# Gates turned four units at a time on VectorE, b2's product over 128 zero-padded rows, TensorE's inserted transposes grouped

## The reference

```
HW   = layernorm(x) @ W                       # (8, 2048, 128)
A    = relu((adj + adj.T) / 2)                # (2048, 2048), symmetric
d    = A.sum(axis=1) ** -0.5
x1   = x + relu((I - d[:,None] * A * d[None,:]) @ HW)
z    = layernorm(x1)
p    = softmax(z @ router_w.T)                # 8 experts, the best 2 kept, made to sum to 1
out  = x1 + z + sum_e p_e * (gelu(z @ w1[e] + b1[e]) @ w2[e] + b2[e])
```

## Time and profile before

| | before |
|---|---|
| median of 3 | 950.52 us (948.55 to 951.11) |
| profiled execution | 949.63 us, span 947.9 us |
| mean granted TensorE clock | 0.986 of 2.4 GHz |
| TensorE products (PE) | 890.9 us busy, 94% |
| VectorE (DVE) | 645.9 us, 68% |
| ScalarE (ACT) | 516.9 us, 55% |
| GpSimd (POOL) | 311.3 us, 33% |
| stages | setup to about 87 us, graph to 542.7 us, experts to the end |

### The profile page before, as it was taken

One profiled execution on the slowest core, in us unless ns is written; L12 is line 12 of the kernel. 1 busy time (PEld: TensorE's weight loads), 2 busy tenths in 40 slices (PEclk: granted clock), 3 DMA queues, 4 the chain that ended last, 5 costly groups with the idle time before them and its releaser, 6 DMA issues.

```text
span 947.9 us, 15352 instructions
## 1 busy us (share of the span) xinstructions
PE 890.9 (94%) x4446; PEld 724.9 (76%) x4446; DVE 645.9 (68%) x1558; ACT 516.9 (55%) x899; POOL 311.3 (33%) x312
## 2 busy tenths in 40 slices
PE   4766799999999999999999989999999999999997
PEld 3765588888888788878888857777777777777775
DVE  3996634756867734152424288888888888888886
ACT  3665332344443321222122287888888888888885
POOL 0689335555574734474433430000000000000000
PEclk9997899999999999999999999999999999999999
DMA  9983255676485336867766774777777777777771
GB/s 286 327 253 125 98 202 212 255 270 215 166 290 175 102 139 251 281 245 262 267 246 239 286 253 163 263 265 266 267 269 270 270 270 270 270 270 270 270 269 45
DMA packets 93022, 222.98 MB, mean 235 GB/s; under 512 B 8856, under 2 KB 59568, under 8 KB 81072
## 3 DMA queue, kind: packets, MB, share of 16 engines
q1 hardware_dynamic: 86752, 211.59, 63.3%
q0 software_dynamic: 2560, 8.39, 2.3%
q10 hardware_dynamic: 3664, 2.43, 1.0%
HBM read 157.89 MB, written 64.49 MB: 235 GB/s over the span
## 4 chain that ended last, share of the span: by engine, by line
PE 81%; DVE 7%; POOL 4%; issue 4%; ACT 3%; DMA 1%; DVEq 0%; ACTq 0%; POOLq 0%
PE bank L913 11%; PE bank L915 11%; PE bank L914 11%; PE bank L1290 6%; PE bank L1293 6%; PE bank L1277 6%; PE bank L1279 6%; PE bank L1278 6%; PE bank L1291 6%; POOL col_sum L543 3%; PE bank L858 2%; PE bank L330 2%; DVE y_lo L699 2%; PE bank L1299 1%; PE bank L1287 1%
## 5 line engine op out<-in xcount | busy, mean ns | idle before, releaser
L1367 DVE TENSOR_TENSOR gated<-c_all,act_h 128x512 f32<-128x512 f32 x256 | 177.7, 694 | 46.2 <-ACT act_h L1329 41.6
L1329 ACT ACTIVATE act_h<-bank,b_sb 128x512 f32<-128x512 f32 x256 | 176.5, 690 | 58.5 <-PE bank L1279 54.0
L1372 DVE TENSOR_TENSOR g_lo<-gated,g_hi 128x512 fp32r<-128x512 f32 x256 | 175.7, 686 | 0.2
L1336 ACT ACTIVATE g_hi<-gated 128x512 fp32r<-128x512 f32 x256 | 159.1, 621 | 4.4 <-DVE gated L1367 4.4
L1262 POOL DMA_DIRECT2D out<-fin x32 | 24.3, 759 | 367.6 <-DVE fin L1380 362.9
L913 PE MATMUL bank<-y_hi,stage 128*128 128x512 f32 x256 | 111.3, 435 | 3.6 <-DVE y_lo L699 3.6
L1002 POOL TENSOR_TENSOR rstd<-var_eps,neg_half 128x4 f32<-128x4 f32 x32 | 48.8, 1525 | 179.5 <-DVE var_eps L1039 179.4
L1277 PE MATMUL bank<-z_e,w_hi 128*128 128x512 f32 x256 | 103.8, 406 | 1.7 <-ACT act_h L1329 1.5
L913 PE MATMUL bank<-y,stage 128*128 128x512 f32 x256 | 104.5, 408 | 0.0
L1293 PE MATMUL bank<-g_lo,w_hi 128*128 128x512 f32 x256 | 101.0, 395 | 2.9 <-DVE g_lo L1372 2.9
L1290 PE MATMUL bank<-g_hi,w_lo 128*128 128x512 f32 x256 | 103.7, 405 | 0.0
(11 more groups left out here) (118 smaller groups left out, 1582.1 us busy)
## 6 DMA issues: line engine op xcount, KB each, us to landing
c_all<-c_scratch SPq DMA_DIRECT2D x64, 1024.0 KB, 8.0
s_scratch<-stage SPq DMA_DIRECT2D x14, 2048.0 KB, 8.4
stage<-s_scratch SPq DMA_DIRECT2D x14, 2048.0 KB, 7.8
z_e<-z_scratch SPq DMA_DIRECT2D x32, 512.0 KB, 7.0
z_scratch<-z_hl SPq DMA_DIRECT2D x31, 512.0 KB, 2.7
x_raw<-in_x SPq DMA_DIRECT2D x32, 256.0 KB, 7.8
x_res<-in_x SPq DMA_DIRECT2D x32, 256.0 KB, 7.1
r_e<-res_scratch SPq DMA_DIRECT2D x32, 256.0 KB, 2.7
```

The source lines that it names most:

```text
L1329: act.activation(v.act_h[e % R][:, :], ps_h[e % 2][:, :], ACT.Gelu, bias=v.b1_sb[:, e:e + 1]).then_inc(gelu_done, 1)
L1336: act.activation(v.g_hi[e % R][:, :], v.gated[e % R][:, :], ACT.Copy).then_inc(hi_done, 1)
L1367: dve.tensor_tensor(out=v.gated[e % R][:, :], in0=v.c_all[s][:, e, :], in1=v.act_h[e % R][:, :], op=ALU.mult).then_inc(gated_done, 1)
L1372: dve.tensor_tensor(out=v.g_lo[e % R][:, :], in0=v.gated[e % R][:, :], in1=v.g_hi[e % R][:, :].bitcast(FP32), op=ALU.subtract).then_inc(lo ...
```

## The change

VectorE turns the gates itself. `gate_parts` is widened from 24 to 32 columns for each group, the last eight set to zero once by GpSimd. After `weigh` has made the gates of a batch, one `transpose` of VectorE turns the whole 128 x 512 tile in squares of 32 x 32 into `gate_x`. There the partitions 32g to 32g+23 hold the gates of the tokens 32g to 32g+31 of each group, so a run of tokens is only 32 long, 128 bytes. Sixteen stores for each batch (four units by four g, each of 24 x 4 runs) bring them to the same `c_dram`. SyncE issues them in unit 7, 11, ..., 31, ahead of `store_unit`, and GpSimd those of the last batch at the start of its expert stage. `turn_gate` and `copy_gate` and their entries in the tail lists are gone.

`b2_parts` and `c_parts` get 128 partitions; GpSimd sets all of them to zero once, in unit 20, and rows 0 to 23 are then filled as before. L1287 runs over 128 rows.

The inserts are moved: groups 0 and 1 from after steps 2 and 4 to after step 2, groups 2 and 3 from after steps 10 and 13 to after step 12, behind `turn_z`; `turn_x` from after steps 1 and 5 to after steps 2 and 6, the second one behind `project`.

```diff
-        v.gate_parts = sb("gate_parts", [P, T, 3 * E], FP32, at)
+        v.gate_parts = sb("gate_parts", [P, T, 32], FP32, at)
-        v.gate_t = [sb(f"gate_t{i}", [3 * E, CW], FP32, at) for i in range(2)]
+        v.gate_x = sb("gate_x", [P, T, 32], FP32, at)
-        v.b2_parts = sb("b2_parts", [3 * E, P], FP32R, at)
+        v.b2_parts = sb("b2_parts", [P, P], FP32R, at)
-        v.c_parts = [sb(f"c_parts{i}", [3 * E, CW], FP32R, at) for i in range(2)]
+        v.c_parts = [sb(f"c_parts{i}", [P, CW], FP32R, at) for i in range(2)]
...
+    def store_gates(eng, batch):
+        eng.wait_ge(gate_turned, batch + 1)
+        for u in range(4 * batch, 4 * batch + 4):
+            rows = v.c_dram[unit(u)].rearrange("e (q g t) -> g e q t", q=Q, g=4)
+            for g in range(4):
+                eng.dma_start(rows[g], v.gate_x[32 * g:32 * g + 3 * E, Q * (u % 4):Q * (u % 4) + Q, :]).then_inc(
+                    gate_last if batch == U // 4 - 1 else gate_out[half(u)], 16)
...
         # SyncE, unit u
+            if u >= 7 and u % 4 == 3:
+                store_gates(sp, (u - 7) // 4)
             if u == U - 2:
                 v.load_first(sp)
             if u:
                 store_unit(u - 1)
...
         def route(u):
-            wait(pe, gate_copied, gates_before[u + 2] if u + 2 <= U else U - 4)
...
         def between(u, i):
-            if ks and i in (1, 5):
-                wait(pe, gate_copied, gates_before[u])
-                pr.turn_x(pe, ks[i // 4])
-            if ks and i in (6, 9):
-                pr.project(pe, ks[i // 9])
-            if ahead and i in S_AT and S_AT.index(i) < st.n_groups(u + 1):
-                st.turn_group(pe, u + 1, S_AT.index(i))
-            if i in (8, 11) and gates_in(u):
-                if ks:
-                    pe.wait_ge(pr.xt_copied, ks[1] + 1)
-                turn_gate(gates_in(u)[i // 11], u - 1)
-            if u and i == 12:
-                turn_z(u - 1)
+            groups = range(st.n_groups(u + 1)) if u + 1 < MB else range(0)
+            if i == 2:
+                if ks:
+                    pr.turn_x(pe, ks[0])
+                for g in groups[0:2]:
+                    st.turn_group(pe, u + 1, g)
+            if ks and i == 6:
+                pr.project(pe, ks[0])
+                pr.turn_x(pe, ks[1])
+            if ks and i == 9:
+                pr.project(pe, ks[1])
+            if i == 12:
+                if u:
+                    turn_z(u - 1)
+                for g in groups[2:4]:
+                    st.turn_group(pe, u + 1, g)
...
-        v.tail_tensor = {0: [(turn_early, U - 6)], 1: [(turn_early, U - 5)], 5: [(turn_z, U - 1)], 7: [(route, U - 1)],
-                         12: [(turn_late, U - 4)], 13: [(turn_late, U - 3)], 14: [(turn_late, U - 2)],
-                         15: [(turn_late, U - 1)]}
+        v.tail_tensor = {5: [(turn_z, U - 1)], 7: [(route, U - 1)]}
...
-        v.tail_scalar = {1: [(copy_gate, U - 6)], 2: [(copy_gate, U - 5)], 6: [(copy_z, U - 1)], 8: [(store_last, U - 1)], 9: [(exps, 7)], 13: [(copy_gate, U - 4)],
-                         14: [(copy_gate, U - 3)], 15: [(copy_gate, U - 2), (copy_gate, U - 1)]}
+        v.tail_scalar = {6: [(copy_z, U - 1)], 8: [(store_last, U - 1)], 9: [(exps, 7)]}
...
         # GpSimd, graph stage
+        pool.wait_ge(v.summed, v.all_groups)
+        pool.memset(v.gate_parts[:, :, 3 * E:], 0.0).then_inc(pad_made, 1)
+            if u == MB + 4:
+                pool.wait_ge(acc_done, MB)
+                v.zero_rows(pool)          # b2_parts, c_parts[0], c_parts[1]
...
         # VectorE, at the end of weigh(batch)
+            dve.wait_ge(gate_done, batch + 1)
+            dve.wait_ge(pad_made, 1)
+            if batch > 4:
+                dve.wait_ge(gate_out[1], 256 * (batch - 4))
+            else:
+                wait(dve, gate_out[0], 256 * batch)
+            dve.transpose(v.gate_x[:, :, :].rearrange("p t c -> p (t c)"),
+                          v.gate_parts[:, :, :].rearrange("p t c -> p (t c)")).then_inc(gate_turned, 1)
...
         # GpSimd, expert stage
+        v.store_gates(pool, U // 4 - 1)
         over_units(pool, store)
```

More of the change, by code:

```diff
@@ L760, in graph_stage @@
     gate_turned = sem("gate_turned")
-    gate_copied = sem("gate_copied")
+    pad_made = sem("pad_made")
     res_out = [sem(f"res_out{h}") for h in range(2)]
     z_out = [sem(f"z_out{h}") for h in range(2)]
-    gate_out = [[sem(f"gate_out{h}{i}") for i in range(2)] for h in range(2)]
+    gate_out = [sem(f"gate_out{h}") for h in range(2)]
+    gate_last = sem("gate_last")
     v.acc_done = acc_done
-    v.half_stores = [[(res_out[h], 16 * MB), (z_out[h], 16 * MB), (gate_out[h][0], 8 * MB), (gate_out[h][1], 8 * MB)]
+    v.half_stores = [[(res_out[h], 16 * MB), (z_out[h], 16 * MB), (gate_out[h], 64 * MB - 256 * h)]
                      for h in range(2)]
+    v.half_stores[1].append((gate_last, 256))
     STEPS_A, STEPS_B = 11, 6
@@ L843, in tensor @@
     def tensor(pe):
-        S_AT = (2, 4, 10, 13)
         def turn_z(u):
@@ L949, in exps @@
             act.activation(v.expo[:, :, :], v.shifted[:, :, :], ACT.Exp).then_inc(exp_done, 1)
-        def copy_gate(u):
-            i = u % 2
-            act.wait_ge(gate_turned, u + 1)
-            if u >= MB + 2:
-                act.wait_ge(gate_out[1][i], 16 * ((u - MB) // 2))
-            elif u >= 2:
-                act.wait_ge(gate_out[0][i], 16 * (u // 2))
-            act.activation(v.gate_t[i][:, :], ps_c[i][0:3 * E, :], ACT.Copy).then_inc(gate_copied, 1)
-            act.wait_ge(gate_copied, u + 1)
-            act.dma_start(v.c_dram[unit(u)], v.gate_t[i][:, :]).then_inc(gate_out[half(u)][i], 16)
         def store_last(u):
@@ L981, in scalar @@
                     pr.high(act, ks[g - 2])
-                if g == 2:
-                    for w in gates_in(u)[0:1]:
-                        copy_gate(w)
                 if ahead and g < st.n_groups(u + 1):
                     st.high_group(act, u + 1, g)
-            for w in gates_in(u)[1:2]:
-                copy_gate(w)
             if u:
@@ L1099, in weigh @@
             gate, high, low = (v.gate_parts[:, :, i * E:(i + 1) * E] for i in range(3))
-            wait(dve, gate_turned, 4 * batch)
+            wait(dve, gate_turned, batch)
             dve.tensor_tensor(out=gate, in0=v.picked[:, :, :], in1=spread(v.inv_top), op=ALU.mult).then_inc(route_step, 1)
@@ L1159, in expert_stage @@
     b2_placed = sem("b2_placed")
+    zero_made = sem("zero_made")
     w_hi_made = sem("w_hi_made")
@@ L1187, in weights_high, with zero_rows @@
         act.wait_ge(b2_in, 32)
+        act.wait_ge(zero_made, 3)
         act.activation(v.b2_parts[0:2 * E, :], v.b2_raw[:, :], ACT.Copy).then_inc(w_hi_made, 1)
+    def zero_rows(pool):
+        for rows in (v.b2_parts, v.c_parts[0], v.c_parts[1]):
+            pool.memset(rows[:, :].bitcast(FP32), 0.0).then_inc(zero_made, 1)
     def weights_low(pool):
@@ L1240, in load_first @@
             sp.wait_ge(stored, count)
+        sp.wait_ge(zero_made, 3)
         load_unit(sp, 0, 0, 0)
```

18 lines of the change are left out of this document (3 added, 15 removed).

## The result

| | before | after |
|---|---|---|
| median | 950.07 us (948.55 to 951.11, 4 runs) | 940.40 us (937.32 to 942.39, 4 runs) |
| profiled execution | 949.63 us, span 947.9 | 942.19 us, span 940.5 |
| mean granted TensorE clock | 0.986 | 0.981 |

The ratio is 0.990 (95% interval 0.986 to 0.993): faster, by 9.7 us where 30 were forecast. 940.4 lies outside the range of 915 to 932.

What follows compares the result with a forecast made beforehand. TensorE was taken to bound both stretches. Gains of 15.0 + 12.0 + 3.3 = 30.3 us, nothing added back, took 949.63 to 919.3, with 0.9 for the median 920.2 us; own range 916 to 924, whole range 915 to 932.

Steps and rivals of the forecast that it cites:

- the term of the stores: SyncE's queue: 16 issues a batch at 0.37 us take 6.0 us, at most 15.8; taken as covered, nothing added.
- the slack of 3.5: Graph stage: the matrix's load lands at 8.8 of a unit's 12.35 us, so 3.5 us of lateness cost nothing.
- point of stall: Graph stage: TensorE stalls once a batch of gate stores occupies the DMA engines for more than 5.5 us.
- It can happen in three batches: Stage loads behind the gate stores of units 19, 23 and 27 could be late; expected cost 0.
- Clogged queues: Rival, chance 0.08: 128-byte runs at twice 0.042 us fill the DMA engines 8.0 us a batch; 7.5 us lost, 928.
- Part 2: Expert stage: b2's product over 128 rows instead of 24 saves 0.40 us in each of 30 units, 12.0 us.
- Part 3: Inserts joined and moved: 0.7 us from joins, 1.3 in unit 0, 1.3 in units 10 and 14; 3.3 us.
- The wait of 5.06 at 106 us: Unit 0, after step 10: TensorE waits for VectorE's y parts; later inserts were to shorten it to about 3.7.
- Part 1: Gate turns leave TensorE: 11.3 us in the graph stage, 0.5 and 3.2 at the experts' start; 15.0 us.
- 0.7 us is covered by the later turn_x: Units 10 and 14: VectorE's new transpose of 0.7 us was to cost nothing, as the turned input comes later.
- the 3.7 us forecast for the start of the experts: Gate turns gone at the experts' start: 0.5 us in the first two steps, 3.2 after steps 12 to 15.

Runs made afterwards that it cites:

- e4: Kernel after, with each of a batch's 16 gate stores writing 24 runs of 512 bytes instead of 96 of 128 (gates at other tokens); 923.23 us.
- e19: Kernel after, with 32 unused columns behind each row of the gates' scratch, so rows lie 544 instead of 512 columns apart; 924.77 us.
- e14: Kernel after, with the stores of two units of each batch in 24 runs of 512 bytes, the other two unchanged (half the gates at other tokens); 925.06 us.
- the spread version: Also called e1: kernel after, with a batch's 16 gate stores issued on SyncE's queue over three units, six, five and five; 923.78 us.
- e17: Kernel after, with the same 96 runs of 128 bytes per store sent to other columns, leaving gaps between rows (gates at other tokens); 924.67 us, one run.
- e5: Kernel before, with only b2's product padded to 128 zeroed rows; 936.62 us.
- e6: Kernel before, with only the moved inserts, gate turns left after steps 8 and 11; 946.09 us.
- e8: The spread version with all inserts back at their old places; 926.95 us.
- e10: The spread version with VectorE's transpose made twice in each batch; 925.33 us.
- e18: Kernel after, with each gate store in 48 runs of 256 bytes that follow at one stride over all rows (gates at other tokens); 940.62 us, one run.
- e2: Kernel after, with the gate stores issued on GpSimd's queue instead of SyncE's, eight in each of two units; 928.14 us.

## Why the prediction was wrong

**The step that failed** is the term of the stores: "One small issue takes 0.37 us in the median, 0.99 at most, so 6.0 us, at most 15.8", and behind it "Covered, and at worst the stage load is 4.4 us late". An issue took 0.79 us and a batch 13.3. The median was taken from a transfer of other shape, and the upper end of 15.8 us, which was written down, wasn't carried into the sum, although 4.4 lies above the slack of 3.5. In the kernel after the stage load of 445.51 comes 4.7 us late (the one before it is issued at 428.50, a unit is 12.3), and lands 4.3 us slower, 9.0 in all against the slack of 3.5: 5.5, of which 4.6 were seen as a wait. The step before it was sound. For the matrix, slack and point of stall were read rightly: holds of 6.9 (e4), 7.6 (e19) and 10.1 us (e14) cost nothing in the second half.

**What the prediction left out behind that step.** First, the batch is also ahead of the input's loads, in units 7 and 11; units 9, 10 and 13 of the kernel after take 2.2, 0.7 and 4.9 us longer than in the spread version. "It can happen in three batches" counted only the stage loads. Second, the transfers that are held back are issued together, and the stage load among them lands after 12.1 us, 9.6 and 9.3 in the three batches; the windows show the DMA engines full in that time (1.03). Why the one behind unit 23 is so much slower than the other two stays open. Third, a wait costs more than its length: the 4.6 us in unit 25 cost 7.6, since the granted clock fell behind it, and it fell in units 13 and 29 too. Together 12.1 + 7.8 us in the profiles, less 0.3 in unit 14 and less 1.5 us that the spread version loses at the start of the experts: that is the gap of 18 us between the spans (940.5 and 922.6).

**Clogged queues** had the right place (L905 waiting for the matrix in units 21, 25, 29) and the wrong mechanism. During the hold the DMA engines weren't full (0.11); SyncE wasn't issuing the loads. The Trainium skill's rule on transfers under 512 bytes (DMA: Bandwidth & Descriptors, section "Specifications") doesn't explain it: e17 has the same 128-byte runs and is 16 us faster. The same page of the Trainium skill, section "Issuing engines are not separate DMA queues", calls the time that the issuing takes "usually small relative to the DMA itself"; here it was 0.79 us for 12 KB, sixteen times in a row, and the whole loss. The measurement decides.

**Part 2**, 12.0 us: the mechanism right, the size low by one. It was worth 13.3 in e5's expert stage, 0.42 and not 0.40 a unit and 0.6 ahead of the third unit, which had been put at nothing. The Trainium skill's rule that 32 rows take the time of 128 (TensorE: Matmul & The Clock Gate, section "Why this matters for your kernels") doesn't cover a 24-row product between 128-row ones; the row of the trace did.

**Part 3**, 3.3 us: right within what can be told; e6 gives 2.8, and e8 against the spread version 3.2, with the clock's fall in it. The wait of 5.06 at 106 us became 3.67.

**Part 1**, 15.0 us: too much by about 4. In the units where TensorE is the bound each pair of gate turns was worth 0.9 us, as read from the earlier trace rows. But where VectorE sets the time they bring nothing and its new work costs: unit 11 takes 17.2 us in the spread version and 16.4 in e6 with a pair of gate turns still in it, unit 14 17.4 and 16.8. That is 0.9 + 0.8 + 0.6 = 2.3 us less than reckoned. The prediction had "0.7 us is covered by the later turn_x". Of the 3.7 us forecast for the start of the experts at most 1.8 came (0.6 of them came in e5 too, by b2's product; the 1.8 are of e4, from the router's product of unit 30 to the third b2 product: 40.7 us before, 39.0 there). The four late gate turns and the wait behind two gate copies are gone, but the transpose has its price there too (0.6 in e10), and TensorE reaches z's transposes sooner and waits for GpSimd. GpSimd's z in before took 4.52 us; after:

```profile
554.38 6.68 POOL L974 TENSOR_SCALAR z<-x,mv,rstd 128x128 f32<-128x128 f32 x4
561.15 1.29 POOL L979 TENSOR_TENSOR res<-x,z 128x512 f32<-128x512 f32 x1
```

In e1 and e19 the clock also fell behind this wait, 0.91 in the mean up to the router's product where e4 had 1.00; there these units lose another 1.6 us and nothing of the gain is left.

**The sum.** Without the held queue the change gives 923 to 925 us, where 920.2 was forecast; the 2.3 and 1.9 us of part 1, less the 0.7 us that part 2 brought beyond its forecast from the third unit on, account for the 3 us. The prediction's mechanism of gain was right, and one cost was mis-sized by a factor of two: 13.3 us of issues where 6.0 were taken, past a slack that 10.1 still fits into.

## What to carry to other kernels

A queue of DMA issues is a resource in time like an engine: price each issue from a row of the same shape, not of the same size, and where the price's upper end reaches past a slack, carry that case into the forecast. When stores in a row issue slowly, look at whether source and destination fold into the same shape; a few unused columns between rows may halve the price. Where a batch of issues is longer than the slack of what stands behind it, split it: e1, with every issue at its high price, came within 0.6 us of e4. And compare profiles unit by unit before one difference of a microsecond is given a cause: a fall of the clock behind the same wait was worth 1.6 us here, and came in one execution and not in the other.

## What the runs showed of the hardware

- An issue on SyncE's queue of 24 rows of 4 runs of 128 bytes takes 0.377 us (e19); the same with the rows' pitch equal to four times the runs' pitch takes 0.787 (after), and 48 runs of 256 bytes in one row of runs 0.784 (e18). On GpSimd's queue the first two are 0.583 and 0.734.
- While SyncE issued sixteen such stores the DMA engines' share was 0.11; the transfers held back then filled them (1.03, 342 GB/s), and a load of 2 MB landed after 12.1 us instead of 7.8.
- The granted clock fell behind a wait of TensorE of 1.87 us in one execution (e5) and not in another (before) with the same instructions around it; unit 14 took 18.7 and 17.1 us.
- GpSimd's four operations of z on 128 x 128 take 3.13 us where VectorE has pauses (second half of e2), and 4.52 and 6.68 at the start of the experts, before and after; in the last case VectorE works without pause. That VectorE's work is the reason was not tried by itself.
- A product of 24 rows between products of 128 rows costs TensorE 0.40 us beyond its interval; padded with zeroed rows it costs one interval of 0.23.
- VectorE's transpose of 128 x 512 in 32 x 32 squares takes 0.711 us, the time of an elementwise pass over 512 columns (0.686).
